# Feed-forward blocks of a four-block network: squares and rotation bank by bank, output projection one step later and in another PSUM bank

## The reference, cut to what matters

```python
def _layer(x, wqkv, qs, ksc, wo, lg, lb, w1, b1, w2, b2):    # twice (DEPTH 2)
    h = shift_token(x)                     # second half of the channels comes from the row before
    q, k, v = split(h @ wqkv)              # 8 heads of 64 each
    q = l2norm(q) * qs; k = l2norm(k) * ksc
    q, k = rotary_xpos(q, k)               # q*cos*scale + rotate_half(q)*sin*scale, k with 1/scale
    o = local_attention(q, k, v)           # windows of 64 queries over 128 keys, masked softmax
    x = x + o @ wo
    h = shift_token(x)
    h = (h - mean(h)) / sqrt(var(h) + 1e-05) * lg + lb
    a, g = split(h @ w1 + b1)              # 341 each
    return x + (a * gelu(g)) @ w2 + b2
...
x = x + _L0_ffn_ref(_layernorm(x), ...)    # this block stands twice in the network
```

## Time and profile before

| what | value |
|---|---|
| median of 3 runs | 5035.81 us (5032.77 to 5036.17) |
| the profiled execution: its own time | 5039.37 us |
| the profiled execution: span from first to last instruction | 5037.7 us |
| PE / DVE / ACT / POOL busy over the span | 79% / 57% / 52% / 34% |
| mean granted TensorE clock | 0.864 of full |

### The profile page before, as it was taken

The page is one execution under the profiler, slowest core; times in us unless marked ns, Lnnn a source line. Parts: engine busy times, 40 slices in busy tenths (PEclk is TensorE's granted clock), DMA queues, the critical chain, the costliest instruction groups (busy, mean ns, idle before and its releaser), DMA issues.

```text
span 5037.7 us, 101534 instructions
## 1 busy us (share of the span) xinstructions
PE 3958.2 (79%) x31924; PEld 2425.0 (48%) x31924; DVE 2871.0 (57%) x5889; ACT 2620.8 (52%) x6422; POOL 1703.7 (34%) x1415
## 2 busy tenths in 40 slices
PE   2999999996688888744666664999999917888886
PEld 1555555553455555522222222777777715555554
DVE  2555555555566676543444443666666656767664
ACT  1555555553566666423333332666666605666664
POOL 0000000000777777523222221111111128777773
PEclk9999999998899999865555555999999959999998
DMA  3222222221101101017999999777777611111111
GB/s 122 78 79 82 78 79 78 84 77 45 44 22 23 24 23 23 16 66 287 382 381 378 381 379 370 260 243 273 242 275 243 227 34 26 23 23 23 23 24 28
DMA packets 373723, 701.02 MB, mean 139 GB/s; under 512 B 53220, under 2 KB 160056, under 8 KB 373608
## 3 DMA queue, kind: packets, MB, share of 16 engines
q1 hardware_dynamic: 329576, 565.25, 32.8%
q0 software_dynamic: 44032, 134.30, 7.3%
HBM read 336.53 MB, written 314.64 MB: 129 GB/s over the span
## 4 chain that ended last, share of the span: by engine, by line
PE 60%; DMA 13%; DVE 7%; issue 7%; POOL 5%; ACT 3%; SPq 1%; DVEq 1%; POOLq 0%; ACTq 0%
DMA rel_k<-b_stage_k 12%; PE ps L332 5%; PE ps L1452 5%; PE ps L340 5%; PE ps L351 5%; PE ps L1461 5%; PE ps L862 4%; PE ps L1443 3%; PE ps L821 3%; PE ps L1472 3%; PE ps L882 2%; PE ps L836 2%; PE ps L847 2%; POOL f_rn L759 2%; PE ps L1344 2%
## 5 line engine op out<-in xcount | busy, mean ns | idle before, releaser
L1368 DVE COPY b_stage_k<-ps 128x640 f32<-128x640 f32 (+2 forms) x512 | 359.3, 722 | 471.1 <-DMA rel_k<-b_stage_k 412.3
L430 ACT ACTIVATE a_p<-a_s,a_min 128x512 f32<-128x512 f32 x512 | 367.1, 718 | 469.6 <-DVE a_min L474 469.6
L1365 ACT ACTIVATE b_stage_q<-ps 128x640 f32<-128x640 f32 (+2 forms) x512 | 316.4, 624 | 506.8 <-PE ps L1347 390.2
L474 DVE CUSTOM_DVE_ANT_0 a_s<-ps,a_table 128x512 f32<-128x512 f32 x512 | 333.5, 689 | 374.4 <-PE ps L332 371.8
L1526 ACT ACTIVATE c_p<-c_s,c_min 128x512 f32<-128x512 f32 x512 | 371.0, 725 | 291.9 <-PE ps L1461 179.8
L1344 PE MATMUL ps<-b_e,b_st_k 48*128 48x512 bf16 (+1 forms) x512 | 305.9, 597 | 263.8 <-DVE b_stage_k L1368 263.8
L1561 DVE CUSTOM_DVE_ANT_0 c_s<-ps,c_rq 128x512 f32<-128x512 f32 x512 | 353.2, 690 | 202.5 <-PE ps L1452 189.8
L188 POOL COPY y<-ln_rows 128x512 f32 x32 | 19.9, 621 | 1305.2 <-DVE ln_rows L180 1305.2
L757 POOL TENSOR_TENSOR f_rot<-f_rc,f_rs 128x1024 f32<-128x1024 f32 x128 | 302.9, 2367 | 354.3 <-DVE f_rs L1017 354.0
L942 ACT ACTIVATE f_p<-f_s,f_min 128x128 f32<-128x128 f32 x1024 | 397.6, 392 | 39.6 <-DVE f_min L1005 35.6
L759 POOL TENSOR_TENSOR f_rn<-f_ss,f_power 128x16 f32<-128x16 f32 x128 | 373.8, 2920 | 14.3 <-DVE f_ss L1026 0.4
(11 more groups left out here) (171 smaller groups left out, 9374.7 us busy)
## 6 DMA issues: line engine op xcount, KB each, us to landing
rel_q<-b_stage_q SPq DMA_DIRECT2D x64, 1280.0 KB, 7.7
rel_k<-b_stage_k SPq DMA_DIRECT2D x64, 1280.0 KB, 7.7
c_rq<-rel_q SPq DMA_DIRECT2D x64, 1024.0 KB, 7.3
c_rk<-rel_k POOLq DMA_DIRECT2D x64, 1024.0 KB, 11.8
a_table<-skew_bias SPq DMA_DIRECT2D x64, 896.0 KB, 4.6
f_vb<-f_v SPq DMA_DIRECT2D x256, 128.0 KB, 2.3
rel_k<-b_stage_k SPq DMA_DIRECT2D x32, 1024.0 KB, 9.4
rel_q<-b_stage_q SPq DMA_DIRECT2D x32, 1024.0 KB, 5.3
```

The lines of the kernel that those rows point to most:

```text
L430: nc.scalar.activation(a_p[:, lt % 2, h, :], a_s[:, lt % 2, h, :], ACT.Exp, bias=a_min[:, lt % 2, h:h + 1], scale=-1.0, accum_out=a_sum[:, ...
L1368: moves_b1(dve, 1, lambda out, src: nc.vector.tensor_copy(out, src))
```

## The change

Four edits, all in the feed-forward phase:

1. Bank by bank. The square of q and k is two ACT instructions (one for each PSUM bank) in place of one, and the rotary products are six DVE instructions in place of three. `f_qk_full`, `f_squared` and `f_turned` count per bank, and PE's transposes of q wait for the q half alone, those of k for the k half.
2. The output projection (`join_heads`) and the addition to `y` work on a new pipeline stage `d`, four steps older than the newest tile, instead of on `c`. On PE the projection moves from the end of a step to just after the projections of the new tile; it writes bank MIXED instead of V_BANK. Waits that guarded MIXED and V_BANK move with it (a new `mixed_free` before the MLP's uses of MIXED).
3. On DVE the addition to `y` moves ahead of the sum of squares; the statistics move behind the reciprocal.
4. The shifted-row copies (SP) move from m = 2 to m = 3, waiting for `d`'s addition; the POOL copy of the other half stays in m = 3 but moves from ahead of the rotary addition to the end of the step.

`mask_and_min` stays where it is, first in DVE's step.

```diff
@@ -597,7 +597,7 @@
     F_ZEROS = 6
-    f_qk_full, f_squared, f_turned = tile_sem("f_qk_full"), tile_sem("f_squared"), tile_sem("f_turned", 3)
+    f_qk_full, f_squared, f_turned = tile_sem("f_qk_full", 2), tile_sem("f_squared", 2), tile_sem("f_turned", 6)
     f_summed, f_ss_ready, f_rn_ready = tile_sem("f_summed"), tile_sem("f_ss_ready"), tile_sem("f_rn_ready")
@@ -652,7 +652,7 @@
             for m in range(LT):
-                step(m, rows(0, m), rows(1, m), rows(2, m), rows(3, m), whole(-1), whole(-2), whole(1))
+                step(m, rows(0, m), rows(1, m), rows(2, m), rows(3, m), rows(4, m), whole(-1), whole(-2), whole(1))
@@ -692,15 +692,15 @@
             if a is not None:
                 sp.dma_start(f_vb[0:WINDOW, (m + 1) % LT, :], f_v[WINDOW:P, m, :]).then_inc(f_vb_loaded[m], 16)
-            if m == 2 and ln is not None:
+            if m == 3 and ln is not None:
                 half = slice(DIM // 2, DIM)
-                hold(sp, f_x_mid, upto(c.g))
+                hold(sp, f_x_mid, upto(d.g))
                 hold(sp, f_hn_ready, upto_b(ln.g - 1, LT))
@@ -747,12 +747,8 @@
                 fetch(nxt)
-            if m == 3 and ln is not None:
-                hold(pool, f_x_mid, upto(ln.g * LT + 3))
-                hold(pool, f_hn_ready, upto_b(ln.g - 1, LT))
-                nc.gpsimd.tensor_copy(f_h[:, :, 0:DIM // 2], y[:, bass.ts(ln.y, LT), 0:DIM // 2]).then_inc(f_h_left, 1)
             if a is not None:
-                pool.wait_ge(f_turned, upto(a.g, 3))
+                pool.wait_ge(f_turned, upto(a.g, 6))
                 pool.wait_ge(f_normed, upto(a.g - 1))
@@ -762,6 +758,10 @@
                    f_rn[:, :].unsqueeze(2).broadcast_to([P, 16, DF]), ALU.mult).then_inc(f_normed, 1)
+            if m == 3 and ln is not None:
+                hold(pool, f_x_mid, upto(ln.g * LT + 3))
+                hold(pool, f_hn_ready, upto_b(ln.g - 1, LT))
+                nc.gpsimd.tensor_copy(f_h[:, :, 0:DIM // 2], y[:, bass.ts(ln.y, LT), 0:DIM // 2]).then_inc(f_h_left, 1)
@@ -778,17 +778,15 @@
             if b is not None and s2 is None:
-                pe.wait_ge(f_squared, upto(b.g))
-                pe.wait_ge(f_turned, upto(b.g, 3))
+                pe.wait_ge(f_squared, upto(b.g, 2))
+                pe.wait_ge(f_turned, upto(b.g, 6))
             pe.wait_ge(f_qT_moved, upto(a.g - 2))
             pe.wait_ge(f_kT_moved, upto(a.g - 2))
-            mm(ps[:, QK, :], h, f_wqkv[:, a.layer, 0:INNER], start=True, stop=True)
+            mm(ps[:, QK, :], h, f_wqkv[:, a.layer, 0:INNER], start=True, stop=True).then_inc(f_qk_full, 1)
             mm(ps[:, QK + 1, :], h, f_wqkv[:, a.layer, INNER:2 * INNER], start=True, stop=True).then_inc(f_qk_full, 1)
         def project_v(a, h):
-            pe.wait_ge(f_x_mid, upto(a.g - 4))
-            if a.first:
-                pe.wait_ge(f_v_moved, upto(a.g - 1))
+            pe.wait_ge(f_v_moved, upto(a.g - 1))
             mm(ps[:, V_BANK, :], h, f_wqkv[:, a.layer, 2 * INNER:3 * INNER], start=True, stop=True).then_inc(f_v_full, 1)
@@ -803,15 +801,11 @@
-        def mix_values(m, c, mlp):
+        def mix_values(c):
             pe.wait_ge(f_v_moved, upto(c.g))
             pe.wait_ge(f_vb_loaded[(c.m - 1) % LT], (c.batch + (2 if c.m > 0 else 1)) * 32)
-            pe.wait_ge(f_oT_moved, upto(c.g - 1))
-            if m == 0 and mlp is not None:
-                pe.wait_ge(f_y_done, upto_b(mlp.g - 1))
-            if m == 1 and mlp is not None:
-                pe.wait_ge(f_hnT_moved, upto_b(mlp.g))
+            pe.wait_ge(f_x_mid, upto(c.g - 1))
             pe.wait_ge(f_pT_moved[0], upto(c.g))
@@ -824,33 +818,44 @@
         def transpose_qk(a, b):
-            if a is not None:
-                pe.wait_ge(f_squared, upto(a.g))
-                pe.wait_ge(f_turned, upto(a.g, 3))
-            else:
-                pe.wait_ge(f_qT_moved, upto(b.g - 1))
-                pe.wait_ge(f_kT_moved, upto(b.g - 1))
             pe.wait_ge(f_normed, upto(b.g))
-            for k, full in enumerate((f_qT_full, f_kT_full)):
+            for k, (full, moved) in enumerate(((f_qT_full, f_qT_moved), (f_kT_full, f_kT_moved))):
+                if a is not None:
+                    pe.wait_ge(f_squared, upto(a.g - 1, 2) + k + 1)
+                    pe.wait_ge(f_turned, upto(a.g - 1, 6) + 3 * k + 3)
+                else:
+                    pe.wait_ge(moved, upto(b.g - 1))
                 for i in range(PAIRS_F):
-        def join_heads(a, c):
-            if a is not None:
-                pe.wait_ge(f_v_moved, upto(a.g))
-            else:
-                pe.wait_ge(f_x_mid, upto(c.g - 1))
-            pe.wait_ge(f_oT_moved, upto(c.g))
+        def join_heads(m, d, mlp):
+            if m == 0 and mlp is not None:
+                pe.wait_ge(f_y_done, upto_b(mlp.g - 1))
+            if m == 1 and mlp is not None:
+                pe.wait_ge(f_hnT_moved, upto_b(mlp.g))
+            if m == 2 and mlp is not None:
+                pe.wait_ge(f_gelued, upto_b(mlp.g, 3))
+            if m == 3 and mlp is not None:
+                pe.wait_ge(f_hid_ready, upto_b(mlp.g, 3))
+            pe.wait_ge(f_oT_moved, upto(d.g))
             for i in range(PAIRS_F):
-                last = mm(ps[:, V_BANK, 0:DIM], f_oT[:, i * P:(i + 1) * P], f_wo[:, c.layer, i, :],
+                last = mm(ps[:, MIXED, 0:DIM], f_oT[:, i * P:(i + 1) * P], f_wo[:, d.layer, i, :],
                           start=(i == 0), stop=(i == PAIRS_F - 1))
-        def turn_normed(c, mlp):
-            if c is None:
-                pe.wait_ge(f_y_done, upto_b(mlp.g - 1))
+        def mixed_free(c, d):
+            if c is not None:
+                pe.wait_ge(f_oT_moved, upto(c.g))
+            elif d is not None:
+                pe.wait_ge(f_x_mid, upto(d.g))
+        def turn_normed(c, d, mlp):
+            mixed_free(c, d)
+            pe.wait_ge(f_y_done, upto_b(mlp.g - 1))
             pe.wait_ge(f_hn_ready, upto_b(mlp.g, LT))
@@ -884,17 +889,19 @@
             h = f_hT[:, m * P:(m + 1) * P]
                 project_v(a, h)
+            if d is not None:
+                join_heads(m, d, mlp)
             if c is not None:
             if c is not None:
-                mix_values(m, c, mlp)
+                mix_values(c)
             if m == 1 and mlp is not None:
@@ -906,15 +913,16 @@
                 scores(b)
-            if c is not None:
-                join_heads(a, c)
             if m == 0 and mlp is not None:
-                turn_normed(c, mlp)
+                turn_normed(c, d, mlp)
             if m == 1 and mlp is not None:
+                mixed_free(c, d)
                 mlp_up(mlp, 1, f_gate_full, (2,))
             if m == 2 and mlp is not None:
+                mixed_free(c, d)
                 mlp_up(mlp, 0, f_value_full, (2,))
             if m == 3 and mlp is not None:
+                mixed_free(c, d)
                 mlp_down(mlp)
@@ -942,12 +950,13 @@
             if a is not None:
-                act.wait_ge(f_qk_full, upto(a.g))
                 act.wait_ge(f_summed, upto(a.g - 1))
-                nc.scalar.activation(f_sq[:, :], ps[:, QK:QK + 2, :].rearrange("p b n -> p (b n)"),
-                                     ACT.Square).then_inc(f_squared, 1)
+                for k in range(2):
+                    act.wait_ge(f_qk_full, upto(a.g - 1, 2) + k + 1)
+                    nc.scalar.activation(f_sq[:, k * INNER:(k + 1) * INNER], ps[:, QK + k, :],
+                                         ACT.Square).then_inc(f_squared, 1)
             if a is not None:
@@ -1008,14 +1016,16 @@
             dve.wait_ge(f_rotated, upto(a.g - 1))
-            dve.wait_ge(f_squared, upto(a.g))
-            tt(f_rc[:, :].rearrange("p (b h d) -> p b h d", b=2, d=DF), qk,
-               cs[:, 0, :, :].unsqueeze(2).broadcast_to([P, 2, HF, DF]), ALU.mult).then_inc(f_turned, 1)
-            out = f_rs[:, :].rearrange("p (b h d) -> p b h d", b=2, d=DF)
-            for h in range(2):
-                to, src = slice(h * 32, h * 32 + 32), slice((1 - h) * 32, (1 - h) * 32 + 32)
-                tt(out[:, :, :, to], qk[:, :, :, src],
-                   cs[:, 1, :, to].unsqueeze(2).broadcast_to([P, 2, HF, 32]), ALU.mult).then_inc(f_turned, 1)
+            for k in range(2):
+                heads = ps[:, QK + k, :].rearrange("p (h d) -> p h d", d=DF)
+                rc = f_rc[:, k * INNER:(k + 1) * INNER].rearrange("p (h d) -> p h d", d=DF)
+                rs = f_rs[:, k * INNER:(k + 1) * INNER].rearrange("p (h d) -> p h d", d=DF)
+                dve.wait_ge(f_squared, upto(a.g - 1, 2) + k + 1)
+                tt(rc, heads, cs[:, 0, k, :].unsqueeze(1).broadcast_to([P, HF, DF]), ALU.mult).then_inc(f_turned, 1)
+                for h in range(2):
+                    to, src = slice(h * 32, h * 32 + 32), slice((1 - h) * 32, (1 - h) * 32 + 32)
+                    tt(rs[:, :, to], heads[:, :, src],
+                       cs[:, 1, k, to].unsqueeze(1).broadcast_to([P, HF, 32]), ALU.mult).then_inc(f_turned, 1)
```

(13 more changed lines are left out.)

## The result

The changed kernel takes 5155.7 us (median of 4, 5152.7 to 5160.1) against 5035.8: ratio 1.024, interval 1.0222 to 1.0258, so 120 us slower where 126 had been forecast. Its profiled span is 5158.0 us. The phases outside the two feed-forward calls agree within 4 us.

What follows compares the result with a forecast made beforehand. No engine is full; a chain across engines sets the pace, 51.9 us per batch. 3.6 us more for 13 batches (47) plus 16 at the edges is 63 per call, 126 for two: 5160 us, range 5105 to 5210.

Steps and rivals of the forecast that it cites:

- The late transfer: Shifted rows issue behind m = 3's value copies; chain fixed at 10.48 us, mask of m = 0 4.6 later.
- The gains in m = 3: In m = 3 the mask starts 1.85 us earlier and mixing at 1508.8 instead of 1511.35; gain 3.2 us.
- m = 0 to m = 2: Late statistics put m = 1's transposes 5.0 us later and m = 2's mixing 4.1 later; batch 55.6 us.
- The edges of a call: First batch with statistics 9 us later, last full one about 5, drain 2: 16 of 63 us per call.
- The range: 5105 to 5210 us, from bounds of transfer (35 us), split (10 us) and chain readings (1.5 us a batch).
- Half clock as a rival: PE's 7 us idle in m = 0 brings half clock, 1.5 us per batch, 48 in all: 5210; chance 9%.
- cover argument: Against half clock costing time: m = 0 has about 9 us of cover under POOL's chain.
- the cost of edit 1: Six rotary instructions instead of three on DVE cost 0.2 us, bounds 0 and 0.5; q transposes start earlier.
- The small loss: Bank-wise work frees DVE and PE earlier in m = 3, or transfers escape the value copies' cost: 5095; chance 7%.
- no change: Gains of m = 3 and m = 0 to 2 cancel the late statistics: 5036 us; chance 3%.
- the two uncollected microseconds of m = 1 and m = 2: The moved projection saves PE 1.0 us in each of m = 1 and m = 2, not collected.
- landing is covered: Statistics don't bind, so the mask of m = 0 starts 4.5 us earlier, 5.2 per batch: 4870; chance 5%.

Runs made afterwards that it cites:

- experiment 1: Changed kernel with the 127-partition shifted-row transfer cut in two, of 112 and 15 partitions: 4953.8 us, ratio 0.9835.
- 3: Changed kernel with SP issuing the shifted rows ahead of the two value copies of m = 3: 5083.7 us, ratio 1.0101.
- experiment 4: Kernel before with only SP's shifted rows moved to m = 3, behind the value copies: 5308.3 us, ratio 1.054.
- experiment 2: Kernel before with the shifted-row transfer cut in two, of 112 and 15 partitions: 5018.4 us, ratio 0.9967.
- experiment 10: Changed kernel with 7 filler matmuls of 512 columns in each m = 0, ahead of the moved output projection: 5162.0 us, ratio 1.0255.
- 11: Changed kernel without the bank-by-bank edit (one square, three rotary instructions, one wait for both): 5172.0 us, ratio 1.0261.
- 12: Changed kernel without the bank-by-bank edit and with 7 filler matmuls in m = 0: 5174.6 us, ratio 1.0281.
- experiment 6: Kernel before with the bank-by-bank edit alone (squares, rotation, transposes): 5085.1 us, ratio 1.0101.
- experiment 7: Kernel before with the bank-by-bank edit alone, plus three filler matmuls in m = 1 and two in m = 2: 5018.6 us, ratio 0.9967.
- experiment 5: Changed kernel with the transfer cut in two and issued first, and POOL's half copied right after the rotary addition: 4893.3 us, ratio 0.9719.
- experiment 9: Changed kernel with 14 filler matmuls of 512 columns in each m = 0, ahead of the moved output projection: 5182.6 us, ratio 1.0286.
- experiment 8: Kernel before with three filler matmuls ahead of the q and k transposes of m = 3: 5009.9 us, ratio 0.9952.

## Why the prediction was right, step by step

*The late transfer*: right, and shown from three sides, by taking the length away (experiment 1), by moving its issue alone (3) and by adding the delay alone (4). Its chain of 10.5 us is the same in all 32 batches; the value copies ahead of it did not stretch it. The issue came 0.35 us later than worked out, since 0.5 us lie between the last value copy and it, not 0.15.

*The gains in m = 3*: right to 0.1 us for mask and mixing. The 152 us between experiment 4 and the changed kernel hold them together with the rest of the change.

*m = 0 to m = 2*: right within 0.4 us. From the mask of m = 0 to POOL's release of m = 1 it took 14.5 us (14.75 forecast, 14.3 before). The longer rotation takes up these 0.2 us, so the addition of `d` ahead of the sum of squares, to which I gave 0.25, costs nothing.

*The edges of a call*: the sum of 63 us per call came out as about 60, with the parts moved. The first batch with statistics cost 8 us, in line with the 9; the last batch and the drain 9 to 10, where 5 + 2 were forecast; the first two batches of a call are about 2 us shorter, which had not been forecast. So the 126 came out right in part because these errors cancel. The range was tighter than its own terms: 35, 10 and 48 us add up to 93, not to the 50 to 55 that were given each way. The drain is serial, so every late transfer shows in full there; experiment 2 says the same of the kernel before.

*Half clock as a rival*: the clock did fall in m = 0, and cost nothing there (experiment 10). The prediction's cover argument, 9 us of POOL's chain, holds for the changed kernel; how far it reaches is limited, as experiments 11 and 12 suggest. But edit 1, to which I gave 0.2 us of DVE and some earlier transposes, costs 50 us by itself in the kernel before, and fillers that bring the clock back remove that (experiments 6 and 7). In the changed kernel the half clock stays out of m = 1 and m = 2. That the moved projection fills PE's gaps there is my reading; no run tests it. That the sum came out right owes something to this, and it was luck: the cost of edit 1 was argued for the pair, never for the edit alone.

*The small loss and no change*: neither the bank-wise edit nor the two uncollected microseconds of m = 1 and m = 2 gave anything back. The 200 and 262 us that experiments 1 and 5 collect against the changed kernel lie nearly all in m = 0, behind the statistics. The rival "landing is covered" had put that world at 4870; experiment 5 reaches 4893.

The Trainium skill ("DMA: Bandwidth & Descriptors", section "Why a DMA increments its semaphore by 16 and not by 1") names 127 partitions as a one-engine case. Experiments 1 and 5 agree: 127 partitions in one piece take 10.5 us from issue to use and move at 16 GB/s, as 112 + 15 they take 3.9, one more issue included, and move at 62. The mean busy share of the 16 DMA engines in those stretches, 0.08 and 0.31, is that of about one engine and of about five.

## What to carry to other kernels

When a stage moves by one step, follow what waits for its last result, above all transfers: their latency doesn't move with them, and the engine whose queue holds the wait takes everything behind it along. Before moving a transfer later, make it short; here one more line was worth 200 us, and the order of two blocks in a queue, changed by itself, 72. And judge an edit that only starts an engine's work earlier by what its idle time looks like afterwards: here two stretches of 3.4 us at half clock in most batches turned an expected gain of 38 us into a loss of 50.

## What the runs showed of the hardware

- A fp32 matmul of 512 columns takes PE 0.86 to 0.87 us at full clock, shown as two instructions of 0.59 that overlap; 14 stood for 12.2 us (experiment 9).
- The half clock can be moved by filler work, and it often doesn't vanish: fillers in m = 3 brought it to m = 0 (experiment 8), fillers in m = 1 and m = 2 left it in m = 3 (experiment 7), and 7 fillers in m = 0 left part of it later in m = 0 (experiment 10). Only 14 fillers in m = 0 left none between 1400 and 2000 us (experiment 9). Idle times of 1.6 and 2.5 us stood ahead of it in experiment 6, while the earlier trace rows has 2.04 us followed by transposes at full speed (1.09 us for 8).
- The issue that follows a one-piece transfer of 127 x 4 rows occupies SP for 6.9 us; after the cut the longest of the three issues usually takes 1.0 us (experiment 5, at most 1.2).
